# Loads of the second sublayer's result in pairs of blocks, GpSimd's scaling moved behind the gathers, and a new order of the middle stage

## The reference

```python
x = x + tanh(g_xattn[0]) * attention(layernorm(x), ctx)            # 32 heads of 128, 8 kv heads
t = layernorm(x).reshape(1024, 512)[:, perm].reshape(1024, 16, 32)  # 1st gated feed-forward
t = einsum('bhd,hdm->bhm', t, up); t = gelu(t); t = einsum('bhm,hmd->bhd', t, down)
x = x + tanh(g_ffn[0]) * t.reshape(1024, 512)[:, argsort(perm)]
xn = layernorm(x)                                                   # 2nd attention-like sublayer
t, p, g = Wt @ ctx, Wp @ xn, Wg @ ctx                               # per block of 128 x 512
att = sum over each group of 16 rows of (p * g)
y = groupnorm(Wz (att * t)) * gn_w + gn_b + ctx
x = x + tanh(g_xattn[1]) * y
x = x + tanh(g_ffn[1]) * expert_of_largest_gate(layernorm(x))       # 8 experts, 512 x 512
```

## Time and profile before

| | |
|---|---|
| median of 3 runs | 787.33 us (785.74 to 789.49) |
| the profiled execution's own time | 792.27 us |
| its span | 790.5 us |
| PE busy | 751.0 us, 95% |
| DVE busy | 455.9 us, 58% |
| ACT busy | 429.6 us, 54% |
| GpSimd busy | 277.7 us, 35% |
| mean granted TensorE clock | 0.978 of full |

### The profile page before, as it was taken

The page is one execution under the profiler, slowest core; times in us unless marked ns, Lnnn a source line. Parts: engine busy times, 40 slices in busy tenths (PEclk is TensorE's granted clock), DMA queues, the critical chain, the costliest instruction groups (busy, mean ns, idle before and its releaser), DMA issues.

```text
span 790.5 us, 12391 instructions
## 1 busy us (share of the span) xinstructions
PE 751.0 (95%) x3847; PEld 589.5 (75%) x3847; DVE 455.9 (58%) x1008; ACT 429.6 (54%) x1274; POOL 277.7 (35%) x439
## 2 busy tenths in 40 slices
PE   5999989899999999999999999999999997987997
PEld 3788877688887878888878788887787643555785
DVE  4785412456465555564655565646558764787653
ACT  4543315556556556555656555655555465557831
POOL 0331005234325333424423523433312457524142
PEclk9999999999999999999999999999999998797999
DMA  8545461132041140140131213203231144664132
GB/s 300 185 134 173 134 190 38 48 157 80 15 174 34 60 175 28 54 187 13 67 140 60 67 44 147 78 14 122 70 114 66 54 147 154 243 256 173 59 108 80
DMA packets 42191, 87.82 MB, mean 111 GB/s; under 512 B 5626, under 2 KB 26106, under 8 KB 38291
## 3 DMA queue, kind: packets, MB, share of 16 engines
q1 hardware_dynamic: 38884, 78.71, 29.1%
q0 software_dynamic: 3248, 8.41, 3.1%
HBM read 70.28 MB, written 35.57 MB: 134 GB/s over the span
## 4 chain that ended last, share of the span: by engine, by line
PE 73%; DVE 5%; ACT 3%; POOL 2%; issue 1%; DMA 1%; POOLq 0%; DVEq 0%
PE banks L915 8%; PE banks L917 7%; PE banks L916 7%; PE banks L949 7%; PE banks L951 7%; PE banks L950 7%; PE banks L901 7%; PE banks L936 3%; PE banks L928 2%; PE banks L1871 2%; PE banks L1870 2%; PE banks L1869 2%; PE banks L960 2%; PE banks L962 2%; PE banks L961 2%
## 5 line engine op out<-in xcount | busy, mean ns | idle before, releaser
L595 ACT ACTIVATE p_sb<-p_sb,nmax 128x128 f32<-128x128 f32 x256 | 99.7, 391 | 57.5 <-DVE nmax L806 57.4
L590 ACT ACTIVATE oT_hi<-banks 128x512 fp32r<-128x512 f32 x64 | 38.2, 596 | 134.6 <-PE banks L962 134.6
L843 DVE SCALAR_TENSOR_TENSOR x_sb<-banks,tgates,x_sb 128x512 f32<-128x512 f32 x64 | 48.0, 750 | 63.5 <-PE banks L951 63.4
L706 POOL TENSOR_TENSOR v_lo<-v_raw,v_hi 128x128 fp32r<-128x128 f32 x64 | 29.4, 460 | 127.7 <-ACT v_hi L638 127.7
L801 DVE SCALAR_TENSOR_TENSOR p_sb<-banks,q_rstd,mask 128x128 f32<-128x128 f32 x256 | 71.5, 342 | 2.9 <-POOL q_rstd L83 2.4
L711 POOL TENSOR_TENSOR p_sb<-p_sb,rsum 128x512 f32<-128x512 f32 x64 | 66.5, 1039 | 15.1 <-DVE rsum L833 15.1
L901 PEld LDWEIGHTS banks<-kT,qT_sb 128*128 128x128 f32 x512 | 67.6, 193 | 5.4
L901 PE MATMUL banks<-kT,qT_sb 128*128 128x128 f32 x512 | 68.1, 276 | 0.0
L790 DVE TENSOR_TENSOR oT_lo<-banks,oT_hi 128x512 fp32r<-128x512 f32 x64 | 44.1, 689 | 32.8 <-ACT oT_hi L590 32.7
L400 PE MATMUL banks<-w_hi,ctx_hi 128*128 128x512 f32 x128 | 54.0, 422 | 8.9 <-DVE ctx_lo L331 8.9
L833 DVE RECIPROCAL rsum<-prob_sum 128x4 f32<-128x4 f32 x64 | 11.3, 176 | 81.8 <-ACT p_sb L595 81.8
(11 more groups left out here) (280 smaller groups left out, 1895.9 us busy)
## 6 DMA issues: line engine op xcount, KB each, us to landing
sorted_x<-in_empty SPq DMA_DIRECT2D x8, 2064.0 KB, 10.5
w_raw<-in_wq_l SPq DMA_DIRECT2D x8, 1024.0 KB, 5.7
w_raw<-in_wo_l SPq DMA_DIRECT2D x8, 1024.0 KB, 4.8
exp_w<-in_exp_w_l SPq DMA_DIRECT2D x8, 1024.0 KB, 9.1
kT_scr<-kT_st SPq DMA_DIRECT2D x16, 256.0 KB
v_scr<-v_st SPq DMA_DIRECT2D x16, 256.0 KB, 2.4
xs<-sorted_x SPq DMA_DIRECT2D x15, 258.0 KB, 3.0
v_raw<-v_scr SPq DMA_DIRECT2D x14, 256.0 KB, 2.6
```

What stands on the lines that cost most here:

```text
L595: last = act.activation(p_sb[:, b % 2, h * P:(h + 1) * P], p_sb[:, b % 2, h * P:(h + 1) * P], ACT.Exp, bias=nmax[:, b % 2, h:h + 1], accum ...
```

## The change

Six things are edited in `middle`, and two instructions move into the attention's start:

1. `tw` and `tb` are made by DVE at the start of the attention instead of the middle stage.
2. SP loads `yU` in four loads of two blocks each (pairs), the first two behind the first third's scatters, where it was one load for each third.
3. GpSimd scales blocks 0 to 3 behind the first gather and 4 to 7 behind the second; nothing stands between the first four scatters. As the target `ctx_res` lies where attention buffers were, it waits for the attention's last `values` product.
4. The group mean and `gate_c` work of PE and DVE stands ahead of the first transposition and update, followed by one `g_product` and 12 matmuls that nobody reads (`WARM`).
5. Transpositions and g products stand in a new order on PE; DVE does all eight updates first and then all eight products.
6. ACT centres blocks 0 to 5 before the updates, and normalises in smaller steps; GpSimd has one `add_ctx` between the last two `rstd3`.

```diff
+            dve.tensor_tensor(s.tw[:, :], s.gn_w[:, :], s.tgates[:, 1:2], ALU.mult).then_inc(s.cols_set, 1)
+            dve.tensor_tensor(s.tb[:, :], s.gn_b[:, :], s.tgates[:, 1:2], ALU.mult).then_inc(s.cols_set, 1)
             dve.tensor_copy(s.mT[:, :], oT_ps[:, 0:P]).then_inc(mT_copied, 1)
...
+        WARM = 12
...
-            for c, (lo, hi) in enumerate(THIRDS):
-                sp.wait_ge(scattered[c], 16 * KT)
-                sp.dma_start(yU[:, :, lo * P:hi * P], d.yT_scr[c].rearrange("(k p) n -> p k n", p=P))\
-                    .then_inc(yU_ld[c], 16)
+            for i in range(B // 2):
+                c = max(i - 1, 0)
+                if i != 1:
+                    sp.wait_ge(scattered[c], 16 * KT)
+                lo = THIRDS[c][0] * P
+                tok = slice(i * QTOK, (i + 1) * QTOK)
+                sp.dma_start(yU[:, :, tok], d.yT_scr[c][:, tok.start - lo:tok.stop - lo].rearrange("(k p) n -> p k n", p=P))\
+                    .then_inc(yU_ld[i], 16)
...
-            def normalise3(c):
-                act.wait_ge(xshift3_done, c + 1)
-                for b in range(*THIRDS[c]):
+            def normalise3(*bs):
+                for b in bs:
+                    act.wait_ge(xshift3_done, 1 if b < HB else b // 2)
                     reached(act, p_done, b - HB + 1)
...
-            for b in range(5):
-                copy_g(b)
+            copy_g(0)
+            copy_g(1)
+            centre(0, 1)
+            copy_g(2)
+            centre(2, 3, 4, 5)
+            copy_g(3)
+            copy_g(4)
             seed3(0)
             copy_g(5)
+            normalise3(0, 1)
+            seed3(1)
+            normalise3(2, 3)
             copy_g(6)
-            normalise3(0)
-            seed3(1)
-            centre(0, 1)
-            normalise3(1)
+            seed3(2)
+            normalise3(4)
             copy_g(7)
-            seed3(2)
-            centre(2)
-            normalise3(2)
-            centre(3, 4, 5, 6, 7)
+            normalise3(5, 6, 7)
+            centre(6, 7)
...
             gather(0)
+            pool.wait_ge(ctx_nat_ld, 16)
+            pool.wait_ge(s.cols_set, 2)
+            pool.wait_ge(s.pv_done, UNITS)
+            pool.wait_ge(s.picked_done, UNITS // HG)
+            scale_ctx(range(4))
             gather(1)
-            pool.wait_ge(ctx_nat_ld, 16)
-            pool.wait_ge(col_step, 2)
-            scale_ctx(range(2))
+            scale_ctx(range(4, B))
             gather(2)
-            scale_ctx(range(2, 4))
             for jt in range(KT):
                 scatter(0, jt)
-                scale_ctx(range(4 + jt, 5 + jt))
...
             rstd3(1)
-            add_ctx(4, 5)
+            add_ctx(4)
             rstd3(2)
-            add_ctx(6, 7)
+            add_ctx(5, 6, 7)
...
-            updates_with_stats(dve, s, update_x, x_done, bn_done, mv_done, xval3_done, THIRDS[:1])
-            negate_mean(0)
             dve.wait_ge(gmean_done, 1)
+            dve.tensor_copy(s.gmean[:, :], sm_ps[:, 0:B]).then_inc(dev_step, 1)
...
+            dve.tensor_scalar(s.nmean[:, :], s.gmean[:, :], -1.0, None, ALU.mult).then_inc(col_step, 1)
...
-            updates_with_stats(dve, s, update_x, x_done, bn_done, mv_done, xval3_done, THIRDS[1:2])
-            negate_mean(1)
-            product(0)
-            updates_with_stats(dve, s, update_x, x_done, bn_done, mv_done, xval3_done, THIRDS[2:3])
-            negate_mean(2)
-            for b in range(1, B):
+            for c in range(3):
+                updates_with_stats(dve, s, update_x, x_done, bn_done, mv_done, xval3_done, THIRDS[c:c + 1])
+                negate_mean(c)
+            for b in range(B):
...
             def transpose_y(b):
-                pe.wait_ge(yU_ld[0 if b < HB else b // 2 - 1], 16)
+                pe.wait_ge(yU_ld[b // 2], 16)
```

More of the change, by code:

```diff
@@ L486, in attention @@
         s.stage_sems = m.sems
+        s.pv_done, s.picked_done = pv_done, picked_done
         s.q_done, s.o_done, s.acc_done, s.pT_lo_done, s.oT_lo_done = q_done, o_done, acc_done, pT_lo_done, oT_lo_done
@@ L1043, in middle @@
         scattered = [m.sem(f"yT_scattered{c}") for c in range(3)]
-        yU_ld = [m.sem(f"yU_ld{i}") for i in range(3)]
+        yU_ld = [m.sem(f"yU_ld{i}") for i in range(B // 2)]
         z_done, z_copied = s.z_done, s.z_copied
@@ L1153, in centre @@
             def centre(*bs):
-                act.wait_ge(col_step, 3)
+                act.wait_ge(col_step, 1)
                 for b in bs:
                     act.activation(s.z[:, b, :], s.z[:, b, :], ACT.Identity, bias=s.nmean[:, b:b + 1]).then_inc(centred, 1)
-            for b in range(5):
-                copy_g(b)
+            copy_g(0)
[5 more added lines that the diff above has]
+            copy_g(4)
             seed3(0)
             copy_g(5)
+            normalise3(0, 1)
+            seed3(1)
+            normalise3(2, 3)
             copy_g(6)
-            normalise3(0)
-            seed3(1)
-            centre(0, 1)
-            normalise3(1)
+            seed3(2)
+            normalise3(4)
             copy_g(7)
-            seed3(2)
-            centre(2)
-            normalise3(2)
-            centre(3, 4, 5, 6, 7)
+            normalise3(5, 6, 7)
+            centre(6, 7)
             act.wait_ge(att_step, 2)
@@ L1257, in z_stats @@
                 dve.bn_aggr(s.zmv[:, b, :], zbn[:, b, :]).then_inc(zmv_done, 1)
-            dve.tensor_tensor(s.tw[:, :], s.gn_w[:, :], s.tgates[:, 1:2], ALU.mult).then_inc(col_step, 1)
-            dve.tensor_tensor(s.tb[:, :], s.gn_b[:, :], s.tgates[:, 1:2], ALU.mult).then_inc(col_step, 1)
             dve.wait_ge(xseed_done, 3)
@@ L1294, in product @@
                                          accum_out=row[:, b:b + 1]).then_inc(row_done, 1)
-            updates_with_stats(dve, s, update_x, x_done, bn_done, mv_done, xval3_done, THIRDS[:1])
-            negate_mean(0)
             dve.wait_ge(gmean_done, 1)
+            dve.tensor_copy(s.gmean[:, :], sm_ps[:, 0:B]).then_inc(dev_step, 1)
+            dve.wait_ge(zmv_done, B)
+            dve.wait_ge(dev_step, 1)
+            dve.tensor_scalar(s.nmean[:, :], s.gmean[:, :], -1.0, None, ALU.mult).then_inc(col_step, 1)
+            dve.tensor_tensor(dev[:, :], s.zmv[:, :, 0], s.gmean[:, :], ALU.subtract).then_inc(dev_step, 1)
+            dve.wait_ge(dev_step, 2)
+            dve.tensor_tensor(dev[:, :], dev[:, :], dev[:, :], ALU.mult).then_inc(dev_step, 1)
+            dve.wait_ge(dev_step, 3)
+            dve.tensor_tensor(dev[:, :], dev[:, :], s.zmv[:, :, 1], ALU.add).then_inc(dev_step, 1)
             dve.wait_ge(s.gate_ld, 16 * GATE_LOADS)
@@ L1419, in _ @@
             pe.wait_ge(yT_copied, PACKS)
-            for b in range(HB):
-                transpose_y(b)
             pe.wait_ge(zmv_done, B)
@@ L1427, in _ @@
             pe.matmul(sm_ps[:, 0:B], s.group_mean[:, :], s.zmv[:, :, 0], start=True, stop=True).then_inc(gmean_done, 1)
-            for b in range(2, 6):
-                g_product(b)
+            g_product(2)
+            for i in range(WARM):
+                pe.matmul(s.ps[4][:, 0:P], s.ident[:, :], s.wgT[:, :], start=True, stop=True)
+            for b in range(HB):
+                transpose_y(b)
+            g_product(3)
             transpose_y(4)
             transpose_y(5)
+            g_product(4)
+            g_product(5)
+            transpose_y(6)
+            transpose_y(7)
             g_product(6)
             p_product(0)
-            transpose_y(6)
-            transpose_y(7)
             g_product(7)
-            p_product(1)
-            p_product(2)
-            p_product(3)
+            for b in range(1, HB):
+                p_product(b)
             pe.wait_ge(dev_step, 4)
@@ L1957, in flamingo @@
         s.exp_b_split, s.exp_b_stored = m.sem("exp_b_split"), m.sem("exp_b_stored")
-        s.ctx_nat_ld = m.sem("ctx_nat_ld")
+        s.ctx_nat_ld, s.cols_set = m.sem("ctx_nat_ld"), m.sem("cols_set")
         s.mid_ld, s.z_done, s.z_copied = m.sem("mid_ld"), m.sem("z_done"), [m.sem(f"z_copied{i}") for i in range(2)]
```

9 lines of the change are left out of this document (removed).

## The result

| | before | changed |
|---|---|---|
| median, first runs (14 each) | 787.41 us (785.74 to 792.62) | 791.03 us (789.26 to 793.54) |
| ratio | | 1.0033, 95% interval [1.0018, 1.0049] |
| profiled execution | 792.27 us | 791.97 us |
| its span | 790.5 us | 790.2 us |
| DVE starts the first update | 670.81 | 678.03 |

What follows compares the result with a forecast made beforehand. PE idling for a DMA load, then slow PE work at half clock holding up DVE, bounded the middle stage. About 4.7 (wait), 0.5 (earlier first update) and a looser chain give -7.5: 787.33 to 779.8 us, range 776.5 to 783.8.

Steps and rivals of the forecast that it cites:

- GpSimd's list: On GpSimd: second and third gathers not moved, scalings 0.76 us each, first third's last scatter near 657.3, was 661.07.
- Rival C: Eight scalings on GpSimd cost 2.15 us each, delaying pair 3; kernel slower by 4.6 us, 791.9; chance 0.04.
- The packs are unchanged: Stretch of small products ahead of the transpositions: taken as unchanged, with two g products behind it ending at 665.16 us.
- PE's list behind the packs: PE before first transposition: ten small matmuls 1.0, one g product 0.9, new matmuls 2.8 us; first transposition at 669.7.
- The updates and what holds them: DVE from its first update: updates over after 12.3 us, last product ends after 18.1 us, at 688.4.
- The second wait of 4.74 us: DVE's wait for block 4's transposition, between its updates of x: goes, about 4.7 us of the gain.
- rival D: Something held for hidden (ACT's centring, GpSimd's additions) brings DVE's second wait back elsewhere: -3 us, 784.3; chance 0.08.
- rival B: Hand-overs behind DVE's updates, or late pair 3: last product ends 20 us after first update, -5.9, 781.4 us; chance 0.16.
- Clock 1.00 from 660 to 690: PE's granted clock stays full in all windows from 660 to 690 us, as PE has no idle stretch.
- rival A: PE's clock falls all the same, not being dense around 662 to 666: first update 673.6, -4.5 us, 782.8; chance 0.12.
- The experts' stage: Stage from the attention column to the end: moved as a whole, its 92 us changing by no more than 1 us.
- From the profiled execution to the median: Same -7.5 us taken off the profiled execution (792.27 to 784.8) and off the median 787.33, giving 779.8.

Runs made afterwards that it cites:

- gap kernel: Changed kernel with two of the eight scalings between third gather and first scatter; ratios to before 0.9917, 0.9921, 0.9908 on chips 14, 9, 6; 1.0064 on chip 15.
- the control on the next chip: Changed kernel once more, nothing edited, on chip 9 beside the kernel before: 782.8 us, ratio 0.9913.
- the control on chip 15: Changed kernel once more, nothing edited, in the second group of runs on chip 15: 789.69 us in one run.

## Why the prediction was wrong

*GpSimd's list: right.* Second and third gather 639.33 and 648.62 (forecast 639.38 and 648.61), a scaling 3.01 / 4 = 0.75 us (0.76), last scatter of the first third 657.52 (657.3). Rival C, slow scalings, is out. The last scatter of all started at 672.20 instead of 668.5, as the scatters had to wait for the late copies.

*"The packs are unchanged": the step that failed.* +7.6 us in the first runs, 0.0 on chip 9 (21.39 in both kernels). I took it as given since no instruction of theirs was edited; what stands beside them was. None of the rivals named it. The trace of before had a small form of it, which the prediction doesn't use. Timeline of PE, then of ACT, of the kernel before:

```profile
642.61 1.37 PE L1393 MATMUL banks<-xg,up 32*128 32x512 f32 x8
645.09 3.77 ACT L1150 ACTIVATE hid<-banks 128x1024 f32<-128x1024 f32 x4 [1.38 <-PE banks L1393]
```

ACT starts 1.1 us behind the end of these eight records, where on chip 9 it starts 0.1 us ahead of it (643.49 against 643.61). It shows in the length too, 22.73 us of packs against 21.39, but only once an undisturbed chip is there to compare with. On such a chip the step held: 21.39 us for both kernels on chip 9.

*PE's list behind the packs: right.* I had 669.7 for the first transposition, 6.45 us behind the packs' end; it was 6.40 in every profile of the changed kernel. The dummies took 2.84 (2.8). I had the first update 7.05 behind the packs' end; it was 7.04.

*The updates and what holds them: right where pair 3 was in time, and that was partly luck.* Forecast 18.1 from the first update to the last product's end; 17.58 in the first runs, 17.72 on chip 6. The second wait of 4.74 us is gone in every profile of the changed kernel, so rival D is out. But on chip 9 it is 19.68, since pair 3 came late, the second form of rival B (S + 20). PE's timeline there:

```profile
674.53 1.49 PE L1359 MATMUL banks<-ident_sb,xT 128*128 128x128 f32 x8 [2.00 <-DMA xT<-yT_scr]
```

The clock then stood at half from 675.09 to 678.50. On chip 6 the same wait of 1.94 left the clock full and cost nothing. The gap kernel shows both too: 17.99 with a full clock on chip 9, 20.39 and 20.42 with a fall near 675 on chips 14 and 6. What was wrong in my sum is how early the last scatter starts: I had it 1.8 us before the first update, it was 0.5 and 0.3 on chips 9 and 6, where the packs are 1.3 us shorter than in my rows and GpSimd's list is not. In the first runs it was 5.8, because most scatters went out while the packs were held up; so pair 3 had time there, and 17.58 came out.

*Clock 1.00 from 660 to 690: wrong in the first runs,* but not for rival A's reason: it had fallen in the packs. The small products and dummies ran at full clock. On chip 9 it fell too, at 675.09, behind the wait for pair 3.

*The experts' stage: right;* "the rest" differs by 0.33 us.

*From the profiled execution to the median: a second error.* The sum was right for a pair of profiled executions: on chip 9 the spans are 789.04 and 781.25, -7.8. But I took 7.5 off a median of 787.33, while the profiled execution had taken 792.27, more than all but one of the 14 of before. It shows an execution in which the clock fell in the first wait. Of the runs of before, 22 of 42 on chip 15 have a mean granted clock of 0.985 or more, and 4 of 38 on chips 14, 9 and 6 (3 of 9 on chip 5). Those four took 785.55 to 787.61 us, the other 34 took 788.39 to 792.74. The medians of the two kinds lie 3.1 us apart on chip 15 and 4.5 on the three others. So about half of before's executions on chip 15 seem to lack some 3 us of what the change takes away. An estimate for the first runs, from these rows: 791.03 - 7.6 = 783.4 without the packs' loss, a gain of 4.0 on 787.41 instead of 7.5. That it is the clock of this stage that holds in those executions isn't shown; the mean is over the whole execution, and none of them was profiled.

On chips of the undisturbed kind the forecast's size is met: -7.5 us (790.33 to 782.8) and -9.0 us (790.89 to 781.89). In absolute time they lie 3.0 and 2.1 us above 779.8, since before starts higher there. No kernel tried was faster than before on chip 15.

## What to carry to other kernels

Lengths from one phase's unchanged instructions are no constants when the change moves DMA work beside them; compare them first when a result is off. Place the profiled execution among the timed ones before its waits are subtracted from a median: if it is one of the slow ones, part of what is cut is not in the median. And run the unchanged kernel as a control beside each variant, on the same chip: a variant alone on one chip (0.9917) seemed to prove a theory that the control on the next chip overturned.

## What the hardware showed unexpectedly

- PE's signals to ACT and DVE can come several us behind the end of the matmuls' records, while ACT's and DVE's own are on time: DVE's copies start 4.50 and 7.38 us behind their products in the first runs, 6.84 in the control on chip 15, and three signals of transpositions came there within 0.12 us. Found here in the stage with GpSimd's indirect DMAs, on the first runs' chip and on chip 15, in a mild form (1.3 us) on chip 5, and not on chips 14, 9 and 6, where the copies follow within 0.28 us.
- On those three chips the packs repeat to 0.05 us (21.39 to 21.44), while medians of one kernel differ between chips by up to 9.6 us (changed: 791.46 and 781.89).
- 24 matmul records that nobody reads, 2.84 us, moved the first update by nothing (7.04 us behind the packs with them, 7.05 without, where PE waits 2.04 us for a load). With them the 16 transposition records behind took 2.16 us, without them 3.63 at half clock; the two kernels differ in GpSimd's list as well.
- A wait of PE for a load of 2.00 us was followed by a fall of the clock on chip 9, one of 1.94 us in the same place on chip 6 was not.
